# Test-time-training layer after a convolution: 64-byte pieces for the block spreads, separate folds and spreads for turned K and Q, two transfers issued by ScalarE, new orders on every engine

## What is computed

```python
x = x + conv3x3(relu(gn(x) * mask(gn(x)))) + bias           # first step
xn = ln(gn(x) as 784 tokens of 128 channels)                 # second step
XQ, XK = rope(xn @ q_w.T), rope(xn @ k_w.T); XV = xn @ v_w.T # 8 heads of 16
eta = token_idx * sigmoid(xn . lr_w + lr_b) / 16
for each chunk of 16 tokens (49 chunks, in turn, state W1, b1 per image and head):
    Z1 = xk @ W1 + b1
    grad = ln_l2_bwd(Z1, xv - xk)
    Attn1 = tril(xq @ xk.T)
    b1_bar = b1 - tril(eta) @ grad
    Z1_bar = xq @ W1 - eta * Attn1 @ grad + b1_bar
    W1 = W1 - (last_eta * xk).T @ grad
    b1 = b1 - sum(last_eta * grad)
    out = xq + ln(Z1_bar)
x = x + ln(out) @ o_w.T
```

## Time and profile before

| what | value |
|---|---|
| median of 3 runs | 2133.62 us (2129.63 to 2134.75) |
| profiled execution, its own time | 2131.73 us |
| its span, first to last instruction | 2129.9 us |
| PE busy | 1804.8 us, 85% |
| DVE, POOL, ACT busy | 1553.4, 1336.7, 1166.9 us |
| DMA queue of SP | 1148384 packets, 143.57 MB, 53.6% of 16 engines |
| mean granted clock of PE | 0.632 of full speed |

### The profile page before, as it was taken

One profiled execution on the slowest core, in us unless ns is written; L12 is line 12 of the kernel. 1 busy time (PEld: TensorE's weight loads), 2 busy tenths in 40 slices (PEclk: granted clock), 3 DMA queues, 4 the chain that ended last, 5 costly groups with the idle time before them and its releaser, 6 DMA issues.

```text
span 2129.9 us, 81338 instructions
## 1 busy us (share of the span) xinstructions
PE 1804.8 (85%) x33518; PEld 1429.6 (67%) x33518; DVE 1553.4 (73%) x3818; ACT 1166.9 (55%) x2554; POOL 1336.7 (63%) x1479
## 2 busy tenths in 40 slices
PE   2868898715898988989989899998998989989887
PEld 1434454304777877778778787777777877778775
DVE  6989988416777777777777777777777777777764
ACT  2324545435556565566665556656566566565653
POOL 1253444474767776677766777667776777676763
PEclk9988999855556565555555555556555555555655
DMA  5085899843454545545455454464554545545444
GB/s 222 1 44 48 102 78 77 77 143 45 57 70 57 76 65 62 72 57 75 65 61 75 57 74 66 59 77 57 72 68 58 76 62 67 70 56 77 60 57 51
DMA packets 1148753, 148.76 MB, mean 70 GB/s; under 512 B 1128416, under 2 KB 1141984, under 8 KB 1148384
## 3 DMA queue, kind: packets, MB, share of 16 engines
q1 hardware_dynamic: 1148384, 143.57, 53.6%
HBM read 40.71 MB, written 38.54 MB: 37 GB/s over the span
## 4 chain that ended last, share of the span: by engine, by line
PE 59%; DVE 11%; ACT 8%; issue 6%; SPq 6%; DMA 6%; POOL 3%; ACTq 0%; POOLq 0%; DVEq 0%
PE p_kt L1604 11%; PE p_m L1617 8%; PE p_x L1632 7%; ACT work L820 7%; PE p_y L1674 6%; PE p_y L1632 6%; PE p_x L1656 5%; SPq L494 4%; PE p_j L1571 3%; PE p_j L1572 3%; DMA late<-work 3%; PE p_j L1573 2%; DMA xs_scratch<-work 2%; PE p_x L1623 2%; SPq L415 2%
## 5 line engine op out<-in xcount | busy, mean ns | idle before, releaser
L1604 PE MATMUL p_kt<-fold,kqk 128*128 128x16 f16 x6272 | 237.0, 180 | 143.9 <-ACT work L820 139.5
L1604 PEld LDWEIGHTS p_kt<-fold,kqk 128*128 128x128 f16 x6272 | 224.5, 117 | 183.1 <-issue 177.9
L820 ACT ACTIVATE work<-p_kt 128x256 f16<-128x256 f32 x392 | 256.6, 785 | 127.2 <-PE p_kt L1604 126.7
L1286 DVE TENSOR_TENSOR work<-work 128x256 f16<-128x256 f32 x196 | 147.8, 857 | 58.0 <-ACT work L801 58.0
L1632 PEld LDWEIGHTS p_x<-w,late 128*128 128x128 f16 x4704 | 178.1, 118 | 11.8
L1632 PEld LDWEIGHTS p_y<-w,late 128*128 128x128 f16 x4704 | 177.6, 118 | 11.1
L1656 PEld LDWEIGHTS p_x<-work,kqk 128*128 128x128 f16 x4704 | 172.2, 118 | 17.6 <-issue 13.2
L596 POOL TENSOR_TENSOR w<-wst,w 128x256 f16<-128x256 f32 x98 | 71.9, 734 | 175.2 <-ACT w L849 175.2
L1617 PE MATMUL p_m<-work,late 128*128 128x16 f16 x4704 | 164.4, 181 | 18.7 <-DVE lgt L1265 10.0
L1507 PE MATMUL p_j<-work 128*128 128x392 f16 x864 | 160.0, 347 | 22.4 <-DVE work L1101 20.7
L1617 PEld LDWEIGHTS p_m<-work,late 128*128 128x128 f16 x4704 | 160.8, 118 | 21.0 <-issue 10.8
(11 more groups left out here) (171 smaller groups left out, 4638.7 us busy)
## 6 DMA issues: line engine op xcount, KB each, us to landing
kqk<-work SPq DMA_DIRECT2D x392, 64.0 KB, 3.3
late<-work SPq DMA_DIRECT2D x392, 64.0 KB, 3.2
late<-work SPq DMA_DIRECT2D x392, 32.0 KB, 2.2
out_y<-work SPq DMA_DIRECT2D x49, 256.0 KB, 6.1
x_scratch<-late SPq DMA_DIRECT2D x24, 392.0 KB, 11.8
xs_scratch<-work SPq DMA_DIRECT2D x24, 392.0 KB, 6.3
work<-x_scratch SPq DMA_DIRECT2D x49, 192.0 KB, 3.2
work<-xs_scratch SPq DMA_DIRECT2D x48, 192.0 KB, 3.2
```

Of the source, the lines that this page charges most:

```text
L820: last = act.activation(kqt16[:, o, g, :, :, :, :].rearrange("p q t e a -> p q (e a) t"), p_kt[:, o * SC:(o + 1) * SC].rearrange("p (q f t ...
L1286: last = dve.tensor_tensor(paired(hl16[:, c % 2, at, g:g + GP, :, :, :, 1]), in_pairs(qk[:, o, :]), paired(hl16[:, c % 2, at, g:g + GP, :, ...
L1604: mm = pe.matmul(p_kt[:, at:at + CS], part, fold16[:, :], start=True, stop=True)
```

## The change

Four things change, all in the scan.

1. Layout: the halves of one head stand by themselves. A piece of a spread is now 16 elements by 2 halves = 64 bytes, and there are twice as many pieces. ACT and DVE write float16 elements 4 bytes apart, without a split into pairs of heads.
2. The turned K and the turned Q are folded, copied and spread apart. `fold_k(s)` makes K of both groups of a step (32 products, fills `p_kt`), `fold_q(s)` Q; `kt_copy(s)` and `qt_copy(s)` are one instruction each, of 512 columns. `kt_spread` and `qt_spread` are 8 DMAs each of 32 KB, with semaphores of their own. `k_dot_q` and `z_state` wait for K's alone, `outputs` for Q's too.
3. `y_store` and `xr_load` (three DMAs in a turn) are issued by ACT in place of SP.
4. The orders of all engines are new. `o_square` has a buffer of its own (`sqo`), and a number of semaphore waits are added on small buffers (`zs`, `osm`, `xh`, `gr`, `ostd`), so that the new orders are safe. The number of products, of vector operations and of bytes stays what it was; ACT has 4 copies of 512 columns a turn in place of 8 of 256.

```diff
-        mbd = second.cut([NG, NP, GB, CS, 2, 2], F16)
+        mbd = second.cut([NG, NH, GB, CS, 2], F16)
...
-        hl16 = scan.cut([2, 2, NG, NP, HD, 2, 2], F16)
+        hl16 = scan.cut([2, 2, NG, C, 2], F16)
...
             def kq_spread(c):
...
-                part = hl16[:, c % 2, :, :, :, :, :, :].rearrange("p o g q d e a -> p (o g q) (d e a)")
+                part = hl16[:, c % 2, :, :, :, :].rearrange("p o g (h d) a -> p (o g h) (d a)", d=HD)
...
+            def turned_spread(c, o, landed_sem):
+                part = kqt16[:, o, :, :, :, :].rearrange("p g h t a -> p (g h) (t a)")
+                whole = ktqt[c % 2][:, o, :, :, :, :, :].rearrange("p g h b t a -> p (g h) b (t a)")
+                for b in range(GB):
+                    at = slice(b * CS, (b + 1) * CS)
+                    sp.dma_start(whole[at, :, b, :], part[at]).then_inc(landed_sem, 16)
+
             @guard_chunk
             def kt_spread(c):
-                sp.wait_ge(kt_copy_done.sem, kt_copy_done.count("group1", 2 * c + 1))
+                sp.wait_ge(kt_copy_done.sem, kt_copy_done.count(2 * c + 1))
+                if c < 2:
+                    sp.wait_ge(s_kt_zero[c], 1)
+                else:
+                    sp.wait_ge(z_done.sem, z_done.count(2 * c - 3))
+                    sp.wait_ge(k_dot_q_done.sem, k_dot_q_done.count(c - 2))
+                turned_spread(c, 1, kt_landed.sem(c))
...
             def turn(k):
+                m_spread(k - 4)
+                kt_spread(k - 3)
+                qt_spread(k - 3)
+                kq_spread(k - 2)
                 xs_next(k)
-                xr_load(k - 5)
-                kq_spread(k - 2)
-                y_store(k - 6)
-                m_spread(k - 3)
-                kt_spread(k - 2)
...
+            def turned_copy(s, o):
+                g = GP * (s % 2)
+                return act.activation(kqt16[:, o, g:g + GP, :, :, :].rearrange("p g h t a -> p g a (h t)"),
+                                      p_kt[:, :].rearrange("p (g a n) -> p g a n", g=GP, a=2), ACT.Copy)
...
-                for o in range(2):
-                    last = act.activation(kqt16[:, o, g, :, :, :, :].rearrange("p q t e a -> p q (e a) t"),
-                                          p_kt[:, o * SC:(o + 1) * SC].rearrange("p (q f t) -> p q f t", f=4, t=CS), ACT.Copy)
...
             def z_square(s):
                 act.wait_ge(z_done.sem, z_done.count(s))
-                if s >= 2:
-                    act.wait_ge(o_sum_done.sem, o_sum_done.count(s - 2))
+                if s >= 1:
+                    act.wait_ge(z_sum_done.sem, z_sum_done.count(s - 1))
...
+            def y_store(c):
+                act.wait_ge(final_done.sem, final_done.count(2 * c + 1))
+                act.dma_start(out[:, :, CS * c:CS * (c + 1)].rearrange("b c n -> c b n"), xr[:, c % 2, :, :]).then_inc(y_stored.sem(c), 16)
...
+            def fold_k(s):
+                if s % 2 == 1:
+                    pe.wait_ge(kt_copy_done.sem, kt_copy_done.count(s - 1))
+                elif s >= 1:
+                    pe.wait_ge(qt_copy_done.sem, qt_copy_done.count(s - 1))
...
+            def fold_q(s):
+                if s % 2 == 0:
+                    pe.wait_ge(kt_copy_done.sem, kt_copy_done.count(s + 1))
+                else:
+                    pe.wait_ge(qt_copy_done.sem, qt_copy_done.count(s - 1))
...
             def turn(k):
+                z_state(2 * k - 6)
+                out_project(2 * k - 10)
+                k_dot_q(k - 3)
+                z_state(2 * k - 5)
                 project(2 * k - 1)
-                z_state(2 * k - 5)
-                fold_kq(2 * k - 4, 0)
+                outputs(2 * k - 7)
...
```

More of the change, by code:

```diff
@@ L28 @@
 FRONT = B - GB
-NP = NH // 2
 CONV_SCALE = 256.0
@@ L282, in program @@
         kt_landed = landed("kt_blocks", 2, GB)
+        qt_landed = landed("qt_blocks", 2, GB)
         m_landed = landed("m_blocks", 1, GB)
@@ L300, in program @@
         target_done = step("target")
-        fold_done = steps("fold", "group0 group1")
-        kt_copy_done = steps("kt_copy", "group0 group1")
+        fold_k_done = step("fold_k")
+        fold_q_done = step("fold_q")
+        kt_copy_done = step("kt_copy")
+        qt_copy_done = step("qt_copy")
         k_dot_q_done = step("k_dot_q")
@@ L489, in kt_spread @@
                     sp.wait_ge(o_done.sem, o_done.count(2 * c - 3))
[L490 to L494 removed]
+                turned_spread(c, 0, qt_landed.sem(c))
             @guard_chunk
@@ L800, in qk_high @@
                     at = o if c % 2 == 1 else 1 - o
-                    last = act.activation(paired(hl16[:, c % 2, at, g:g + GP, :, :, :, 0]), in_pairs(qk[:, o, :]), ACT.Copy)
+                    last = act.activation(hl16[:, c % 2, at, g:g + GP, :, 0], pair(qk[:, o, :]), ACT.Copy)
                 last.then_inc(qk_high_done.sem, 1)
@@ L925, in turn @@
+                w_high(2 * k - 6)
+                qt_copy(2 * k - 3)
+                g_high(2 * k - 5)
                 post_copy(2 * k - 8)
-                b_high(2 * k - 6)
                 x_square(2 * k)
-                ln_root(2 * k)
-                o_square(2 * k - 6)
-                g_high(2 * k - 5)
-                qk_high(2 * k - 1)
+                o_square(2 * k - 6)
+                qk_high(2 * k - 1)
+                post_root(2 * k - 7)
+                o_root(2 * k - 6)
+                b_high(2 * k - 5)
@@ L933, in _ @@
+                ln_root(2 * k)
+                z_square(2 * k - 4)
+                w_high(2 * k - 5)
+                z_root(2 * k - 4)
+                post_norm(2 * k - 7)
+                rate_gate(k - 1)
+                m_high(k - 2)
+                xr_load(k - 3)
+                x_square(2 * k + 1)
+                z_square(2 * k - 3)
             for k in range(NCH + 5):
@@ L1450, in turn @@
                 z_sum(2 * k - 4)
+                post_shift(2 * k - 7)
+                o_inverse(2 * k - 6)
+                z_inverse(2 * k - 4)
+                ln_inverse(2 * k)
+                z_hat(2 * k - 4)
+                final(2 * k - 8)
+                norm(2 * k)
+                z_rate(2 * k - 4)
+                m_mask(k - 2)
+                o_hat(2 * k - 6)
+                g_means(2 * k - 4)
+                rope_cos(2 * k)
+                g_along(2 * k - 4)
+                g_centre(2 * k - 4)
@@ L1692, in turn @@
             def turn(k):
+                z_state(2 * k - 6)
+                out_project(2 * k - 10)
+                k_dot_q(k - 3)
+                z_state(2 * k - 5)
                 project(2 * k - 1)
-                z_state(2 * k - 5)
-                fold_kq(2 * k - 4, 0)
+                outputs(2 * k - 7)
                 post_turn(2 * k - 9)
                 rate_project(k - 1)
-                fold_kq(2 * k - 4, 1)
+                fold_k(2 * k - 4)
                 out_project(2 * k - 9)
-                fold_kq(2 * k - 3, 0)
-                fold_kq(2 * k - 3, 1)
+                fold_k(2 * k - 3)
+                grad(2 * k - 6)
+                fold_q(2 * k - 4)
+                project(2 * k)
                 post_turn(2 * k - 8)
-                project(2 * k)
+                fold_q(2 * k - 3)
                 outputs(2 * k - 6)
-                grad(2 * k - 6)
-                out_project(2 * k - 8)
                 grad(2 * k - 5)
-                k_dot_q(k - 2)
-                z_state(2 * k - 4)
-                outputs(2 * k - 5)
             for k in range(NCH + 5):
```

300 lines of the change are left out of this document (152 added, 148 removed).

## The result

The changed kernel takes 2013.42 us (median of 4 runs, 2006.20 to 2015.91), the kernel before 2132.75 beside it on the same chip: a ratio of 0.9436, 95% interval 0.9409 to 0.9464. Forecast were 2031 us. The number is close, but most of the account behind it isn't what happened.

A forecast was written before the change was run, and what follows sets the result against it. PE was taken to bound: 29.9 us a turn, plus 0.15 for the first pair and 0.65 for turned K and ACT lateness, 30.7; 107 us gained over 48 turns, 5 lost in the fill, 2031 us, range 1985 to 2105.

The forecast's parts named there:

- `y_store`'s landing: Sign on the new ACT queue: the output store would land within 7 us.
- the DMA share of 84%: Sign on the DMA engines: a share near 84%, from 25.7 us of work a turn.
- so does their rate: PE's products: 48 of 16 columns still take 1.60 us, 33.3 ns each, so PE's floor stays 29.9 us a turn.
- rival on the clock: PE's clock rises from 0.56, wide products halve, the turned K's chain of 29.5 us binds: 1974 us; chance 0.06.
- Folds and copies: ACT's copies out of `p_kt`: 0.80 us each, covered by other PE work except 0.1 to 0.15 us at the first pair.
- handover stall of 2.87 us: PE's idle time a turn before three of four folds, waiting for ACT's copy out of `p_kt`, in the kernel before.
- copies no faster: Rival: ACT's copy in its new form costs 1.33 us, a turn of 31.55, 2072 us; chance 0.12.
- The spreads: SBUF-to-SBUF DMAs: 64-byte pieces at 14.5 ns, 25.7 us of DMA work a turn, below the turn, so not the bound.
- The DMAs bind: Rival: at 19.2 ns a piece the DMA engines need 31.7 us a turn, 2079 to 2103 us; chance 0.15.
- slower than before: Rival: a 64-byte SBUF piece costs over 20.2 ns, PE waits for landings every turn; at 24.5 ns 2404 us; chance 0.08.
- SP's order: SP's queue of spread issues: the chains to `z_state` and the first fold both fit, with 0 to 1 us to spare.
- The fill: Start of the scan before the first `k_dot_q`: one more stage after `kq_spread`, 5 us lost.

The follow-up runs named there:

- The best version: Changed kernel with K and Q alone back in head pairs (128-byte pieces), turned K, turned Q and m in 64-byte pieces: 1945.71 us, ratio 0.9125.

## Why the prediction was right, and where it wasn't

The time was right within 0.9%, the direction and the range too. By its own last paragraph the forecast's mechanism was wrong: PE is idle for 5.4 us a turn, not for at most 1.5, and busy for 25.2, not 29.9. The turn came out at 30.67 us against 30.7 because two errors cancel, which is luck. Of the signs that it named, the turn, the copy's row and `y_store`'s landing (6.4 us) came; the DMA share of 84% and the idle time ahead of the folds under 0.5 us didn't.

**The products: wrong.** The step that failed is "so does their rate". The prediction treated 33.3 ns as the price of a product, and it was the price of reading 8-byte steps. The trace of before had rows that could have warned, and the prediction didn't look at them: `rate_project` (L1587) reads its weights, the tokens in `xs_in`, at 4-byte steps. Here are the loads of its weights and those of `k_dot_q` (ns, min/median/max):

```profile
L1587 PEld LDWEIGHTS p_m<-wl,work x588: 96/97/151, 463.4 to 2037.2; 128*128 128x128 f16 x196
...
L1617 PEld LDWEIGHTS p_m<-work,late x4704: 110/118/133, 504.0 to 2087.6; 128*128 128x128 f16 x196
```

The same number of weights is loaded in 97 ns there and in 118 at 8-byte steps. (Its moving operand has 8 columns and not 16, so the row was a hint and no proof.) The experiment with the kernel before and 4-byte steps shows it alone: 25 to 28 ns, with 1.33 us for 48 even at a clock of 0.50. The floor fell from 29.9 to 25.2 us, and 4.3 of these 4.7 come with the step alone (25.6 in that experiment), with what the clock gave there (0.59 in place of 0.56); the 608 products by themselves account for 3.8 to 4.1. The small rest wasn't taken apart. The prediction's rival on the clock took it to rise with PE's pauses gone; it rose from 0.56 to 0.62 while PE was idle more than before.

**Folds and copies: right.** The copy was taken at 0.80 us and measured 0.750; the handover stall of 2.87 us is gone, as ACT keeps PE waiting ahead of the folds for 4.2 us in the whole run. The version with the old layout adds that the order would have done it with copies of 1.34 us too: only 23.7 us of PE's idle time in the run were for ACT. The rival "copies no faster" took 1.0 us a turn for such copies; it is at most 0.5 (23.7 over 49 turns). ACT, forecast near 19.5 us a turn, is busy for 16.0 (its issues not counted), as its other writes in halves got shorter too; it wasn't the bound.

**The spreads: mis-sized.** Forecast were 25.7 us of DMA work a turn, measured is a share of 0.60 (windows row above), 18.4 us of 30.67. The rest was 7.1, so 1280 pieces an engine took 11.3 us: 8.8 ns each, not 14.5, and outside the range of 12.9 to 19.2. A stretch of the changed kernel with little else under way, 1045 to 1053 us, gives 8.8 too (39.7% of 16 engines, 5758 packets); beside ACT's loads, from 1022.5 to 1031.8 us, it is 11.3 (52.2%, 6886 packets). The pieces took 10.3 us in twice the size. The Trainium skill ("DMA: Bandwidth & Descriptors", Why small descriptors are slow (HBM only)) says that transfers from SBUF to SBUF don't suffer the penalty of small descriptors; the trace agrees but for 1.0 us a turn, which isn't told apart from what other transfers do. The nearest rows were wrong: stores to DRAM at 64 bytes don't price a piece that stays in SBUF. "The DMAs bind" and "slower than before" fell with that.

**SP's order: the step that decided.** The prediction put `m_spread` at 6.29, `kt_spread` and `qt_spread` at 5.72 each, and `kq_spread` at 6.7, all by rows of 128-byte pieces in a kernel whose SP had pauses: 24.4 us, by which SP would have 6 us free. They took 5.9, 14.4 and 9.3 in the turn above (the last two 13.9 and 8.5 on average), and the xs loads 1.4 on top, which it left out; with the gaps between, the whole turn. With the old layout the same 34 issues sum to 27.0 us a turn, about 1 more than 24.4 and the xs loads; with 64-byte pieces they sum to 30.4, so 3.4 us come with the smaller pieces. The prediction asked what these cost the DMA engines, and not what they cost the queue that issues them. Single issues show how. This is the chain that ended last, in a later turn, six issues of `kq_spread` in a row, the 0.04 us between some of them left out (start us, us):

```profile
1145.39 0.60 SPq L479
1146.03 0.67 SPq L479
1146.75 0.84 SPq L479
1147.63 1.79 SPq L479
1149.46 0.67 SPq L479
1150.17 1.88 SPq L479
```

Four stand at the floor or little above, two take 1.8 and 1.9 us. The two waits on PE follow from that queue: the turned K is late for `z_state` by 1.9 us a turn, of which the prediction had named the mechanism and sized it at most at 1, and K and Q by 3.0, for which it had left 0 to 1 us to spare.

**The fill: wrong sign.** `k_dot_q` begins at 495.0, 9 us earlier than before and not 5 later; it is 495.6 with the old layout and 501.7 in the kernel before with 4-byte steps, so the new orders bring most of it. The drain is 43 us where 45.5 were taken. Against the 2028 us of the sum, these 14 and 2.5 us are what is left of the difference in the span, 2010.2.

**The sum as it was,** of the turns from 700 to 1700 us: 25.5 of work (831.32 us of 1000), 3.0 and 1.9 of waits for landings, 0.2 of smaller ones (4.8 and 2.4 us in 1000): 30.67.

What stays open: what exactly an issue waits for when it takes over its floor. It goes with its own pieces (1.03 us with 1024, 0.76 with 512) and with what is under way, on its own queue (the reload behind the store, 4.42 us against 0.34, though the DMA engines were full there too) and on others (`kq_spread` beside four loads of ACT, 1.20 us against 1.03), and it happens where the DMA engines are nearly full (a share of 0.92 from 1009.2 to 1013.7 us of the changed kernel, behind `y_store`) as well as at a mean share of 0.69 (`kq_spread`, 1022.5 to 1031.8). Which limit that is, a depth of the queue or the engines' own pace, no run here separates. Nor were the new orders and the separate folds tried one without the other, so their 136 us are not divided.

## What to carry to other kernels

Sum the queue that issues DMAs as you sum an engine, and with durations from a place where it is as full, and its pieces as many, as they will be: 34 issues of 0.6 us at their floor took 31 us here, and the queue went from having pauses to being the bound. Take the mean of an issue and not its median. When a rate has stood still in every row that you read, ask what it is the rate of, and look for a row that differs: here a 16-column product had the price of its weights' stride, and a layout that halves the stride is worth about 4 us a turn on TensorE, but costs pieces on the queue. The best version took the layout only where TensorE gains more than the queue pays: 1945 us, 3.4% below the changed kernel and 8.8% below the kernel before.

## What the runs showed of the hardware that was not expected

- Weights of 128 columns in halves: 118 ns a load at 8-byte steps, 98 to 106 at 4-byte steps (the mean of each line), and 33 to 34 against 25 to 28 ns from product to product. At 8 bytes the granted clock made little difference to it (1.59 us for 48 at 1.00, 1.64 at 0.50), at 4 bytes more (1.20 at 0.94, 1.33 at 0.50). The Trainium skill ("TensorE: Matmul & The Clock Gate", LDWEIGHTS (loading the stationary operand)) gives a load time by the number of columns alone; these rows depend on the step as well, and they decide.
- ScalarE writing 512 columns in halves: 1334 to 1339 ns at 8-byte steps, 750 to 761 at 4-byte steps. With the step went the split into pairs of heads, so the two aren't told apart here.
- A piece of 64 bytes from SBUF to SBUF: about 8.8 ns of an engine (11.3 beside other transfers), half of a 128-byte one (16.1), where stores of 64 bytes to DRAM took 12.9 and 19.2.
- An issue costs its engine 0.34 to 0.63 us when nothing is in the way, and up to 4.86 us right behind a store of 4096 pieces on its own queue. The store itself took 0.38 us from ScalarE and 0.62 from SyncE, its reload 0.34 and 0.62, both at the median; SyncE issues them right behind others there, and its least is 0.38 and 0.34 as well. A spread took 0.59 at least from either.
